# Moving a bf16 copy of the query and key chunks from ScalarE to VectorE in a two-layer transformer kernel

## What is computed

```python
qkv = x @ w_qkv + b_qkv                       # 16 heads of 16
scores = einsum('bhid,bhjd->bhij', q, k) * attn_scale
scores = where(j >= i, scores, -inf)
attn = softmax(scores)                        # layer 0; layer 1 has a sigmoid and a rotary embedding
out = einsum('bhij,bhjd->bhid', attn, v) @ w_out + b_out
x = layernorm(x + out)                        # then the router and the experts of layer 0, then layer 1
```

## Time and profile before

| | us |
|---|---|
| median of 3 runs | 1681.02 |
| lowest and highest run | 1676.84, 1681.13 |
| profiled execution: its own time | 1681.13 |
| span, first to last instruction of it | 1679.4 |
| PE busy | 1401.7 (83%) |
| DVE busy | 909.5 (54%) |
| ACT busy | 706.3 (42%) |
| POOL busy | 495.2 (29%) |

### The profile page before, as it was taken

How to read it: one execution, slowest core, us unless ns; L and a number is a source line. 1 busy time by engine, 2 the same in 40 slices (tenths; PEclk the granted TensorE clock), 3 DMA queues, 4 the chain that set the end, 5 groups by cost and what they waited for, 6 DMA issues and landing times.

```text
span 1679.4 us, 31168 instructions
## 1 busy us (share of the span) xinstructions
PE 1401.7 (83%) x10239; PEld 929.1 (55%) x10240; DVE 909.5 (54%) x3424; ACT 706.3 (42%) x984; POOL 495.2 (29%) x415
## 2 busy tenths in 40 slices
PE   3688898898898639999639999999998749999991
PEld 1245455455454416666424555555555438999991
DVE  1767778878876411111274767766753343344434
ACT  1154555554545310111017577677776512222223
POOL 4032334334344311212210122332221223444442
PEclk7799999999988759999869999999999859999996
DMA  6845436346333022443233656446646324444446
GB/s 168 212 108 105 99 100 143 90 108 146 87 70 114 14 70 76 117 110 82 44 76 79 127 114 142 103 94 131 130 90 167 142 78 67 72 69 70 72 63 213
DMA packets 119549, 174.71 MB, mean 104 GB/s; under 512 B 17623, under 2 KB 101617, under 8 KB 113280
## 3 DMA queue, kind: packets, MB, share of 16 engines
q1 hardware_dynamic: 96320, 148.05, 36.2%
q0 software_dynamic: 20400, 22.37, 8.5%
q10 hardware_dynamic: 2704, 2.70, 0.6%
HBM read 107.64 MB, written 72.69 MB: 107 GB/s over the span
## 4 chain that ended last, share of the span: by engine, by line
PE 61%; DVE 13%; issue 7%; ACT 5%; DMA 4%; POOL 1%; SPq 1%; DVEq 0%; POOLq 0%; ACTq 0%
PE ST L738 8%; PE OT L756 7%; PE ST L1852 7%; PE shared L1864 7%; PE ST L1311 6%; DVE scratch L1145 4%; PE shared L787 4%; PE shared L1510 3%; PE OT L1319 3%; PE shared L1319 3%; ACT arena L877 3%; DMA sum<-arena,block_to_row 1%; PE shared L768 1%; PE shared L1517 1%; PE shared L804 1%
## 5 line engine op out<-in xcount | busy, mean ns | idle before, releaser
L877 ACT ACTIVATE arena<-ST 128x1024 f32<-128x1024 f32 x416 | 413.0, 1024 | 215.1 <-PE ST L738 213.5
L738 PE MATMUL ST<-arena 96*128 96x256 bf16 (+2 forms) x1792 | 248.7, 273 | 42.2 <-DMA arena<-qk_parts 20.7
L756 PE MATMUL OT<-arena,v_aug 128*32 128x256 f32 (+1 forms) x3584 | 249.9, 380 | 4.4 <-POOL arena L1213 1.6
L738 PEld LDWEIGHTS ST<-arena 96*128 96x128 bf16 (+1 forms) x1792 | 150.6, 100 | 150.4 <-ACT arena L877 60.5
L1145 DVE CUSTOM_DVE_ANT_0 scratch<-shared,mask 128x384 bf16<-128x384 f32 (+3 forms) x298 | 135.6, 491 | 47.7 <-PE shared L852 43.7
L1959 POOL DMA_INDIRECT sum<-arena,block_to_row x71 | 111.1, 1565 | 169.6 <-DMA sum<-arena,block_to_row 116.2
L756 PEld LDWEIGHTS OT<-arena,v_aug 128*32 128x32 f32 x3584 | 84.4, 110 | 109.3 <-issue 73.4
L1213 POOL TENSOR_SCALAR_AFFINE_SELECT arena<-arena 128x512 f32<-128x512 f32 (+1 forms) x96 | 78.9, 822 | 217.0 <-ACT arena L877 216.8
L1864 PE MATMUL shared<-arena 128*128 x568 | 134.2, 379 | 0.0
L1681 POOL DMA_INDIRECT slot_x<-x_out,row_to x64 | 63.5, 992 | 165.7 <-DVE keep L1599 148.7
L1145 DVE CUSTOM_DVE_ANT_0 scratch<-ST,mask 128x256 bf16<-128x256 f32 (+3 forms) x214 | 95.4, 479 | 24.8 <-PE ST L852 13.8
(11 more groups left out here) (234 smaller groups left out, 2394.7 us busy)
## 6 DMA issues: line engine op xcount, KB each, us to landing
arena<-qk_parts SPq DMA_DIRECT2D x224, 128.0 KB, 6.9
qk_parts<-qk_src SPq DMA_DIRECT2D x32, 384.0 KB, 2.6
arena<-qk_parts SPq DMA_DIRECT2D x32, 384.0 KB, 4.6
qk_parts<-qk_src SPq DMA_DIRECT2D x64, 192.0 KB, 3.0
arena<-slot_x SPq DMA_DIRECT2D x71, 130.0 KB, 2.4
arena<-qk_parts SPq DMA_DIRECT2D x32, 256.0 KB, 5.3
sum<-x_out SPq DMA_DIRECT2D x16, 512.0 KB, 3.0
arena<-in_experts_inter SPq DMA_DIRECT2D x7, 1024.0 KB, 5.2
```

Source lines behind the costliest of these rows:

```text
L738: mm = pe.matmul(scores[:, i * 256 + at:i * 256 + at + nq], K[par][0:rows, h, kb * P:(kb + 1) * P], Q[par][0:rows, h, q0:q0 + nq], start=T ...
L756: mm = pe.matmul(OT[32 * i:32 * i + 32, q0:q0 + nq], v_aug[par][:, kb, g * GH + i, :], PT[n % RING][:, i, at:at + nq], start=(u == 0), sto ...
L877: act.activation(PT[n % RING][:, :, :], scores[:, :].rearrange("p (h n) -> p h n", h=GH), func, scale=ATT_SCALE).then_inc(L["exp"], 1)
```

## The change

The copy of part 1 (`qk_rest` in bf16, `q2`) is taken from ACT's step `qs` and put behind the subtraction in DVE's step `qs`, with a wait for that subtraction. Before L904 overwrites `qk_flat`, ACT now waits for `q2` of the chunk two before it instead of `rest`.

```diff
@@ a_act
                         order = CHUNKS.index(n)
-                        wait(act, L["rest"], k * 4 + (order - 1))
+                        wait(act, L["q2"], k * 4 + (order - 1))
                         act.activation(qk_flat[order % 2][:, :], bank[:, :], ACT.Identity,
                                        bias=b_qk[:, n:n + 1]).then_inc(free, 1)
-                    elif step == "qs":
-                        order = CHUNKS.index(n)
-                        act.wait_ge(L["rest"], k * 4 + (order + 1))
-                        act.activation(qk_src[n][:, 1, :], qk_rest[order % 2][:, :], ACT.Identity).then_inc(L["q2"], 1)
                     elif step in ("st", "oe"):
@@ a_dve
                         dve.tensor_tensor(rest[:, :], qk_flat[order % 2][:, :], qk_src[n][:, 0, :],
                                           ALU.subtract).then_inc(L["rest"], 1)
+                        dve.wait_ge(L["rest"], k * 4 + (order + 1))
+                        dve.tensor_copy(qk_src[n][:, 1, :], rest[:, :]).then_inc(L["q2"], 1)
```

## The result

The changed kernel takes 1697.17 us (median of 4 runs, 1694.50 to 1699.58), the kernel before beside it 1680.44: a ratio of 1.0111, with a 95% interval of 1.0096 to 1.0127. The change makes the kernel slower by 1.1%. The forecast was 1686 us, 0.3% slower, with a range that ended at 1695.

What follows compares the result with a forecast made beforehand. PE was taken to bound the first 39.4 us of a body slot, DVE the last 25.4. Terms 6.9 + 0.2 + 0.2 - 0.5 - 1.7 = +5.1 us on 1681.13 gave 1686, range 1677 to 1695.

Steps and rivals of the forecast that it cites:

- Fourth chunk: Last chunk in a body slot's DVE-bound part: POOL catches a small DVE operation, 1.37 us late, 5 x 1.37 = 6.9 us.
- First three chunks: Body slots' DVE-bound part: copies hidden in DVE's standstill for POOL, costing nothing; first gains 0.05, first two together -0.1 us.
- The prediction's bound for such catches: Body slots: POOL's moved affine select L1213 may cost or give one standstill, -0.8 to +1.1 us a slot, taken as 0.
- ACT's relief: DVE-bound stretch: exponentials no longer stand behind L909, PE saves up to 2.9 us of waiting; effect on the end 0.
- Clock: Body slots' heads: PE resumes 1.4 us later, so half of 0.7 us low-clock loss returns, 5 x -0.35 = -1.7 us.
- the rival that had the clock give time back: Body slots: second low-clock stretch gone from four slots, 6.8 us back, 3.5 more at heads: 1677.6 us; chance 0.18.
- The third rival: Body slots: earlier L1213 catch one more small DVE operation a slot, +1.1 x 5 = 5.5 us: 1692; chance 0.15.
- Zeroth batch, first and second slot: Before the body slots: +0.2 for the zeroth batch, +0.2 for the first slot, -0.5 us for the second.
- the 3.26 us wait: Second slot: PE waits for ACT's L882, behind L909 and DVE's subtraction; gain taken as 0.5 us, bounds 0 and 1.5.

Runs made afterwards that it cites:

- The extra matmuls: Changed kernel with unit 18's score matmuls issued three times instead of once in each body slot: 1.0023, again 1.0040, of the kernel before.
- third group: Experiments on the third chip, kernel before at 1709 us; the changed kernel, run again unaltered, took 1.0092 of it.
- kernel without any copy: Changed kernel with the copy left out altogether, part 1 staying zero and POOL subtracting behind DVE's subtraction: 1.0010 of the kernel before.
- in another: Body slots' projection steps one to two places earlier: kernel before 0.9911, again 0.9918; changed kernel 0.9930, all against the kernel before in its own order.

## Why the prediction was wrong

- **The range and the time.** It forecast +5 us and measured +17. The mechanism that it named, small DVE operations held by POOL, was right but counted at one chunk of four, and a second one, PE's low clock inside DVE's part, had no term.
- **Fourth chunk: right.** 1.43 us a slot against the 1.37 worked out, shown by the fourth copy alone (1.0033, 5.6 us; 5 x 1.43 is 7.1). Of the 1.43, 0.97 are there even without a copy.
- **First three chunks: the step that failed.** "Three copies of four cost nothing, because DVE already stands still that long for POOL and POOL now starts earlier." It went through POOL's subtraction alone. It said of the first chunk that L1003 is held, "and L1063 follows free"; L1063's counterpart L1059 was held 1.01 us by the affine select that follows POOL's subtraction without a pause. That select, L1213 then, stood at 313.69 in the timeline of before, right behind L1201. The piece grew by 0.77 instead of shrinking by 0.05. At the second chunk L1064 (L1068 before), forecast at its free 0.17, was held 0.57 by the next select. Further on in that piece two more small operations were held where the timeline of before had them free: L1025, 0.58 us, and L1006, 1.08 us (L1083 in other slots), the latter against 0.79 won at L1086, a later one. The prediction's bound for such catches, up to 1.1 a slot, was right in kind, and it took 0.
- **ACT's relief: wrong in kind.** The prediction: "PE has 6 us to spare there, so this moves PE's idle time and not the end: 0." PE's clock fell behind its idle time, and at the lower clock the 6 us were gone: DVE waited 1.49 us in each slot, 7.5 us in all. The extra matmuls, which cut PE's waits in the piece from 2.25 to 1.42 us and took the low stretch and DVE's wait away with it, show that. Whether ACT's relief or DVE's lateness brings the idle time about is not settled: PE idled as long in the piece with ACT's wait put back, and for 1.4 us with ACT free and no copy on DVE.
- **Clock: half of the account.** It forecast -1.7 us, from less of the low stretch at the head behind PE's return. In the second to fifth slot this stretch now ends 3.9 to 4.6 us behind the return instead of 5.2 to 5.5, which at half speed is 0.4 to 0.8 a slot: the 0.7 of which the forecast took half. In the first slot it ends later, and PE's part grew by 0.6. But PE's parts came out 3.9 shorter in sum, and most of it, 1.9 in each of two slots, is where the low stretch some 29 us into the part is gone. That is the mechanism of the rival that had the clock give time back. The low stretch in DVE's part, for which neither had a term, costs more than all this. The third rival, DVE losing more to the affine selects (1692), was the nearest: operations held by the affine selects are seen, but its price (1.1 a slot) lacks the clock's 1.5, and at the first chunk the select catches one because DVE's product comes later, not because the select comes earlier.
- **Zeroth batch, first and second slot: right in sum, by luck.** -0.1 as forecast (+0.2, +0.2, -0.5), but PE's first scores came 0.7 us later (38.27 against 37.57), the scores behind the loads of the earlier trace rows 1.05 later (87.66 against 86.61), where 0.4 was forecast, and the second slot won back 1.2 instead of 0.5. In the zeroth batch three of the four copies were themselves held by POOL, 1.26 us instead of 0.43:

```profile
20.16 1.26 DVE L1122 CAST qk_src<-qk_rest 128x512 bf16<-128x512 f32 x1
...
19.68 1.46 POOL L1199 TENSOR_TENSOR qk_src<-qk_rest,qk_src 128x512 bf16<-128x512 f32 x1 [5.06 <-DVE qk_src L1122]
```

  In the second slot the 3.26 us wait went and two others took its place.
- **In the sum:** forecast 6.9 + 0.2 + 0.2 - 0.5 - 1.7 = 5.1. Measured 7.1 for the fourth chunk, 3.8 for the first, 4.8 for the second, third and their surroundings, 7.5 for DVE's wait for PE, -3.9 in PE's parts, and -1.9 in the rest: 17.4.

The Trainium skill (SBUF — State Buffer, "SBUF: two separate sides") describes the lock as held for one whole GpSimd operation. The trace agrees for each single one (L1059 ends 0.04 us behind L1211). What the prediction lacked was to apply it to every POOL operation of the slot, the affine selects too.

## What to carry to other kernels

When DVE gets more work or POOL gets its operand at another time, lay every POOL operation of the stretch beside every small SBUF operation of DVE, not only the one that the change touches: each that meets cost up to POOL's whole duration here. Slack of TensorE in a stretch that another engine bounds counts at the clock that it will have there; where PE idles just before, as at full banks, half of it may be gone. And before moving work onto the busiest engine, look for a place where that engine waits: the same four copies, with all that they brought, lengthened DVE's part of a slot by 4.7 us in one place and by 0.2 in another.

## What the runs showed of the hardware

- Size does not protect a DVE operation from POOL's lock: a copy of 4 elements a lane that started 0.07 us behind POOL took 1.08 us, and three of the 32 added copies took 1.26 us instead of 0.43, as shown above. The one started at the same moment as POOL was not held, nor was a reduction (L998) that started within L1199.

```profile
320.36 0.18 DVE L998 TENSOR_REDUCE r_s<-r_c 128x4 f32<-128x32 f32 x1
...
333.79 0.17 DVE L1004 TENSOR_SCALAR x_out<-lane 128x4 f32<-128x4 f32 x1
333.86 1.08 DVE L1006 COPY x_out<-r_s 128x4 f32<-128x4 f32 x1
...
333.79 1.12 POOL L1211 TENSOR_SCALAR_AFFINE_SELECT arena<-arena 128x1024 f32<-128x1024 f32 x1 [4.95 <-ACT arena L877]
```

- On three of the four chips ACT stood up to 6 us in PE's part of most body slots for something that the trace does not name (written "remote"), in kernels with and without the change, and such parts were some 1 to 7 us longer; on the first chip no kernel showed it. The row is ACT's waits in PE's part of a slot of the changed kernel, third group:

```profile
ACT arena L877 <- remote: 6.0, 1, 6.0
```

  What it is stays open. It is likely why the kernel before takes 1700 to 1709 us there, but that kernel has no trace from those chips, so this is not shown.
- The same program on the same chip had PE's clock low for 6.8 us in the second to third piece of two slots and for 3.4 us in that of three, with the same instructions and the same 2.25 us of PE's waits for DVE in the piece (the third group's two rows above are one of each). What decides between the two lengths these traces don't fix. In the kernel without any copy, with 1.4 us of such waits, it was 6.8 us in two slots, 3.4 in one and none in two.
